# Order of the value products around the max pass, and one wider mask product, in a two-layer attention and MLP kernel

## What is computed

```python
# layer 1: 16 heads of 32 dimensions, causal, LoRA on q, k, v and o, rotary q and k
scores = where(causal, einsum('bhqd,bhkd->bhqk', Q, K) / sqrt(32), -inf)
x = layernorm(x + multilora(softmax(scores) @ V, Wo))
# layer 2: a second causal attention whose output only steers a small modulation of the gate
mod  = 0.1 * tanh(attention(rmsnorm(x, ln1_w)) @ A)
h    = rmsnorm(x, ln2_w)
gate = silu(h @ W_in.T + mod * (h @ A) @ B)
x    = layernorm(x + x + gate * (h @ W_up.T) @ W_down.T)
```

## Time and profile before

| | |
|---|---|
| median of 3 runs | 2931.94 us (2924.23 to 2940.3) |
| the profiled execution | 2926.47 us, its span 2924.6 us |
| mean granted TensorE clock | 0.965 |
| PE | 2691.6 us busy (92% of the span), 13840 matmuls |
| PEld | 2060.2 us (70%), 13840 loads |
| DVE / ACT / POOL | 1585.8 / 1337.3 / 647.0 us |
| first attention, first batch's first slot to last batch's last | about 72 to 834 us |
| second attention, likewise | about 932 to 1769 us |
| MLP | from about 1800 us on |

### The profile page before, as it was taken

How to read it: one execution, slowest core, us unless ns; L and a number is a source line. 1 busy time by engine, 2 the same in 40 slices (tenths; PEclk the granted TensorE clock), 3 DMA queues, 4 the chain that set the end, 5 groups by cost and what they waited for, 6 DMA issues and landing times. The chain is left out here.

```text
span 2924.6 us, 41449 instructions
## 1 busy us (share of the span) xinstructions
PE 2691.6 (92%) x13840; PEld 2060.2 (70%) x13840; DVE 1585.8 (54%) x4309; ACT 1337.3 (46%) x2755; POOL 647.0 (22%) x528
## 2 busy tenths in 40 slices
PE   5999999999758999999999984999999999999998
PEld 4777777777536667666666653888888888888886
DVE  4777777777635777777776773322222333333333
ACT  2677776767633666666666663211111231111111
POOL 5455555555321122222222111000000000000000
PEclk8999999999867999999999997999999999999999
DMA  5456555555625545555455444211111221111100
GB/s 141 94 132 140 134 127 133 134 131 120 151 85 124 120 97 133 115 104 138 105 111 129 99 76 136 96 45 45 44 44 44 77 84 53 45 46 44 44 29 29
DMA packets 173900, 276.47 MB, mean 95 GB/s; under 512 B 29204, under 2 KB 53524, under 8 KB 173076
## 3 DMA queue, kind: packets, MB, share of 16 engines
q1 hardware_dynamic: 170772, 260.58, 36.9%
q0 software_dynamic: 2304, 12.58, 1.2%
q10 hardware_dynamic: 640, 1.05, 0.1%
HBM read 97.04 MB, written 42.99 MB: 48 GB/s over the span
## 5 line engine op out<-in xcount | busy, mean ns | idle before, releaser
L2222 DVE TENSOR_TENSOR c_product<-c_up_ps,c_gate 128x512 f32<-128x512 f32 x128 | 88.5, 692 | 653.2 <-PE c_up_ps L2288 653.2
L2276 PE MATMUL c_gate_ps<-c_h_split,c_w_split 128*128 128x512 f32 x1536 | 380.3, 396 | 22.6 <-DVE c_w_split L2174 22.6
L2260 PE MATMUL c_down_ps<-c_w_split,c_product_split 128*128 128x512 f32 x1536 | 379.3, 396 | 0.0
L2288 PE MATMUL c_up_ps<-c_h_split,c_w_split 128*128 128x512 f32 x1536 | 378.1, 394 | 0.0
L2276 PEld LDWEIGHTS c_gate_ps<-c_h_split,c_w_split 128*128 128x128 f32 x1536 | 289.0, 188 | 94.8 <-issue 24.4
L2288 PEld LDWEIGHTS c_up_ps<-c_h_split,c_w_split 128*128 128x128 f32 x1536 | 287.9, 187 | 70.5
L2260 PEld LDWEIGHTS c_down_ps<-c_w_split,c_product_split 128*128 128x128 f32 x1536 | 288.5, 188 | 69.0
L278 ACT ACTIVATE b_prob_hi<-b_scores_t_ps 128x384 fp32r<-128x384 f32 (+1 forms) x384 | 200.3, 522 | 235.8 <-PE b_scores_t_ps L268 212.4
L286 DVE TENSOR_TENSOR a_prob_lo<-a_scores_t_ps,a_prob_hi 128x384 fp32r<-128x384 f32 (+1 forms) x384 | 226.5, 593 | 144.0 <-ACT a_scores_t_ps L279 141.3
L2146 ACT ACTIVATE c_gate<-c_gate_ps 128x512 f32<-128x512 f32 x128 | 76.7, 599 | 492.6 <-PE c_gate_ps L2283 492.6
L286 DVE TENSOR_TENSOR b_prob_lo<-b_scores_t_ps,b_prob_hi 128x384 fp32r<-128x384 f32 (+1 forms) x384 | 225.9, 593 | 136.9 <-ACT b_scores_t_ps L279 135.5
(11 more groups left out here) (206 smaller groups left out, 4789.2 us busy)
## 6 DMA issues: line engine op xcount, KB each, us to landing
a_q_stack<-a_q_split SPq DMA_DIRECT2D x192, 128.0 KB, 3.7
a_k_stack<-a_k_split SPq DMA_DIRECT2D x192, 128.0 KB, 3.8
b_q_stack<-b_q_split SPq DMA_DIRECT2D x192, 128.0 KB, 3.3
b_k_stack<-b_k_split SPq DMA_DIRECT2D x192, 128.0 KB, 3.6
c_h_stage<-h_t SPq DMA_DIRECT2D x16, 1024.0 KB, 6.1
c_res<-x SPq DMA_DIRECT2D x16, 1024.0 KB, 5.5
c_w_stage<-in_mlp_w POOLq DMA_DIRECT2D x16, 768.0 KB, 4.5
stage<-in_x_t SPq DMA_DIRECT2D x8, 1024.0 KB, 6.4
```

The costliest lines, as they stand in the source:

```text
L2222: dve.tensor_tensor(product[:, bank, :], up_ps[:, bank, :], gate[:, bank, :], ALU.mult).then_inc(product_done, 1)
L2260: mm = pe.matmul(down_ps[:, t, :], product_split[:, kt % 2, a, t * P:t * P + P], w_split[:, w, kt, 2 * KC * P:], start=(kt == 0 and i == 0 ...
L2276: pe.matmul(gate_ps[:, bank, :], w_split[:, w, ft, c * 2 * P:c * 2 * P + P], h_split[run.pair][:, a, c, :], start=(c == 0 and w == 0 and a ...
L2288: mm = pe.matmul(up_ps[:, bank, :], w_split[:, w, ft, c * 2 * P + P:(c + 1) * 2 * P], h_split[run.pair][:, a, c, :], start=(c == 0 and w = ...
```

## The change

It does two things in the first two stages.

1. `pv_unit` gets a range of passes. All matmuls of a value product but the last are issued directly behind the mask, the last behind the max-pass scores of that slot and ahead of the fill. The order of a unit's key tiles is turned round (`PV_PASSES`): for unit 2 first the two 128-wide matmuls, then the two 256-wide ones.
2. In unit 2 the two key tiles change places in the buffer, so that their diagonal blocks are neighbours; one mask matmul with 256 columns takes the place of two with 128. `colmask` is held twice side by side, at the price of one more DVE copy at the start.

```diff
-KEY_MAJOR = (((0, 0, 512),), ((1, 0, 384),), ((2, 0, 256), (3, 256, 128)))
+KEY_MAJOR = (((0, 0, 512),), ((1, 0, 384),), ((2, 128, 256), (3, 0, 128)))
+DIAGONAL = (P, P, 2 * P)
+PV_PASSES = tuple(tuple((kt, col, width, part) for kt, col, width in unit[::-1] for part in range(2))
+                  for unit in KEY_MAJOR)
...
-    for kt, col, width in KEY_MAJOR[j]:
-        mm = pe.matmul(at.scores_t_ps[:, k % 2, col:col + P], eye_bf[:, :], colmask[:, :],
-                       start=False, stop=True, skip_group_check=True)
-    mm.then_inc(at.score_t_ready, 1)
+    pe.matmul(at.scores_t_ps[:, k % 2, 0:DIAGONAL[j]], eye_bf[:, :], colmask[:, 0:DIAGONAL[j]],
+              start=False, stop=True, skip_group_check=True).then_inc(at.score_t_ready, 1)
...
                     score_t_unit(pe, at, eye_bf, colmask, b, g, slot)
+                    if slot >= 2:
+                        value_needed(b, g, slot - 2)
+                        pv_unit(pe, at, b, g, slot - 2, slice(0, -1))
+                    elif not first:
+                        pv_unit(pe, at, *group(b, g, -1), UNITS - 2 + slot, slice(0, -1))
                     if not (last and g == GROUPS - 1):
                         for k in score_share(slot):
                             score_unit(pe, at, *group(b, g, 1), k)
-                    if slot < 2 and not first:
-                        pv_unit(pe, at, *group(b, g, -1), UNITS - 2 + slot)
+                    if slot >= 2:
+                        pv_unit(pe, at, b, g, slot - 2, slice(-1, None))
+                    elif not first:
+                        pv_unit(pe, at, *group(b, g, -1), UNITS - 2 + slot, slice(-1, None))
...
-                    if slot >= 2:
-                        value_needed(b, g, slot - 2)
-                        pv_unit(pe, at, b, g, slot - 2)
```

More of the change, by code:

```diff
@@ L96, in __init__ @@
         self.eye_bf = sb("eye_bf", [P, P], BF16)
-        self.colmask = sb("colmask", [P, P], BF16)
+        self.colmask = sb("colmask", [P, 2 * P], BF16)
         self.lnw = sb("lnw", [P, 2, KC])
@@ L287, in lo_unit, with pv_unit @@
                       ALU.subtract).then_inc(at.lo_done, 1)
-def pv_unit(pe, at, b, g, k):
+def pv_unit(pe, at, b, g, k, passes=slice(None)):
     h, j = divmod(k, 3)
     n = number(b, g)
-    pe.wait_ge(at.lo_done, n * UNITS + k + 1)
-    if j == 0:
-        at_least(pe, at.pv_copied, n * GH + h - 1)
-    if g == 0 and h == 0 and at.value_steps:
-        pe.wait_ge(at.value_ready, b * at.value_steps[3] + at.value_steps[j])
-    for kt, col, width in KEY_MAJOR[j]:
-        for part, prob in enumerate((at.prob_hi, at.prob_lo)):
-            mm = pe.matmul(at.pv_ps[0:at.vcols, h % 2, kt * P:SEQ], at.value[:, kt, g * GH + h, :],
-                           prob[:, k % at.ring, col:col + width], start=(kt == 0 and part == 0),
-                           stop=(kt == TT - 1 and part == 1), skip_group_check=True)
-    mm.then_inc(at.pv_done, 1)
+    pv = PV_PASSES[j]
+    for kt, col, width, part in pv[passes]:
+        if (kt, col, width, part) == pv[0]:
+            pe.wait_ge(at.lo_done, n * UNITS + k + 1)
+            if j == 0:
+                at_least(pe, at.pv_copied, n * GH + h - 1)
+            if g == 0 and h == 0 and at.value_steps:
+                pe.wait_ge(at.value_ready, b * at.value_steps[3] + at.value_steps[j])
+        prob = (at.prob_hi, at.prob_lo)[part]
+        mm = pe.matmul(at.pv_ps[0:at.vcols, h % 2, kt * P:SEQ], at.value[:, kt, g * GH + h, :],
+                       prob[:, k % at.ring, col:col + width], start=(kt == 0 and part == 0),
+                       stop=(j == 2 and (kt, col, width, part) == pv[-1]), skip_group_check=True)
+        if (kt, col, width, part) == pv[-1]:
+            mm.then_inc(at.pv_done, 1)
 def pv_copy(act, at, b, g, h):
@@ L823, in _ @@
             dve.tensor_copy(eye_bf[:, :], square[:, 0, :]).then_inc(const_ready, 1)
-            dve.tensor_copy(colmask[:, :], square[:, 1, :]).then_inc(const_ready, 1)
+            for i in range(2):
+                dve.tensor_copy(colmask[:, i * P:(i + 1) * P], square[:, 1, :]).then_inc(const_ready, 1)
             def weights(n):
@@ L943, in _ @@
         def _(pe):
-            pe.wait_ge(const_ready, 3)
+            pe.wait_ge(const_ready, 4)
             pe.wait_ge(rows_zeroed, 4)
```

## The result

| | before | after |
|---|---|---|
| median | 2931.62 us of 6 runs (2924.23 to 2940.3) | 2909.63 us of 6 runs (2903.5 to 2917.16) |
| ratio after/before | | 0.9931, interval 0.9914 to 0.9949 |
| profiled execution (span) | 2926.47 us (2924.6) | 2913.56 us (2911.7) |

The change makes the kernel 22 us faster, 0.7%. The forecast was 31 us; 22 lie inside the range. The ratios in this document are those on record and not quotients of the medians (0.9925 here); the two differ by up to 0.001, 3 us.

What follows compares the result with a forecast made beforehand. PE was taken to set the pace. Of 47 us of PE work saved 30 arrive, less 5 for the later max pass, plus 4 and 2 for less waiting: 2931.9 - 31 = 2901 us, range 2883 to 2924 (8 in 10).

Steps and rivals of the forecast that it cites:

- Sign and mechanism: Both attentions: faster, chance 0.78, because a short matmul on PE hides only a narrow weight load.
- Rival 1: Masks on PE: the 0.12 us is the mask's own wherever it stands; 12 us gained, 2920; chance 0.1.
- rival 4: Weight loads on PE: every load is hidden, only the merged mask counts, 1 to 4 us, 2929; chance 0.03.
- Work taken from PE, 47 us: Both attentions: 3.65 us a batch less PE work in the first, 2.66 in the second; 25.6 and 21.3 us.
- The merged mask: Unit 2, both attentions: one 256-wide mask for two saves 0.015 us each, 0.24 us a batch.
- The later max pass, -5 us: Both attentions: max-pass scores come later, delaying DVE's maxima and low part; PE waits at about two places a batch.
- Rival 3: Slots 1 to 7: the later max pass becomes the bound, 76 us lost against at most 47 gained, 2961; chance 0.06.
- What of it arrives, 30 of 47 us: Saved PE work partly becomes waits: a third off the first attention (to 17), four tenths off the second (to 13).
- Rival 2: Both attentions: score buffers and DVE take the saved time back as low-part waits; 9 us gained, 2923; chance 0.1.
- Less waiting, +4 and +2 us: PE's max-pass scores wait less for DVE's buffer (second attention, 4); ACT less for finished heads (first, 2).
- the turning that was forecast: Unit 2's value product turned round and divided: 0.88 us a batch of PE work saved in either attention.

Runs made afterwards that it cites:

- Experiment 5: Changed kernel, but value products of three of four heads in the first attention load 128 columns of weights instead of 65: 2911.01 us, 0.9936 against before.
- repeat: The changed kernel unaltered, run and profiled again later, the same run as experiment 12: 2901.69 us, ratio 0.9923 against before.
- experiment 1: Kernel before with only the merged 256-column mask in unit 2, order of PE as before: 2920.2 us against 2926.04, ratio 0.9975.
- experiment 2: Changed kernel with two 128-wide masks in unit 2 instead of the merged one: 2903.11 us, 0.9924 against before.
- experiment 12: The changed kernel unaltered, measured again beside later runs on the same chip, called the repeat: 2901.69 us, ratio 0.9923 against before.
- experiment 3: Changed kernel with the whole value product ahead of the max pass in both attentions: 2907.55 us, 0.9933 against before.
- experiment 8: Changed kernel, but in slots with a max pass the whole value product stands behind the max-pass scores: 2916.65 us, 0.9943 against before.
- experiment 11: Changed kernel with only the gather of finished heads issued ahead of the next batch's load in the first attention: 2897.5 us, 0.9905 against before.
- Experiment 4: Changed kernel with the key tiles of a value product in their old order: 2912.53 us, 0.9953 against before.
- Experiment 9: Changed kernel, first attention: gather ahead of next batch's load, inverse sums written ahead of the low-rank rows and read back behind them: 2886.45 us, 0.9863 against before.

## Why the prediction was right, and where it wasn't

**Sign and mechanism: right.** The value products behind the mask take the 0.12 us of a mask to 0.07 or 0.08, "0.07 to 0.08 in all slots"; scores of 256 and 128 take 0.18 behind a 256-wide matmul; 13584 matmuls; the MLP alike. Experiment 5 shows the load to be the cause, with the mask unchanged ahead of it. Rival 1 falls, and rival 4 with it. That rule of the Trainium skill (TensorE: Matmul & The Clock Gate, Step-by-step: what each phase is for), that the next weights load while a matmul runs, holds here as far as the running matmul reaches: a 128-column load is hidden behind 256 columns, but 0.05 us of it stick out behind 128.

**Work taken from PE, 47 us: about right, a little high.** The busy time of PE fell by 35.8 us (after) and 41.5 us (repeat). Time gained and waits grown give about the same: in the first attention 9.5 + 7.1 + 3.6 = 20 of the 25.6 us forecast (19 in the repeat), in the second 11.8 + 7.4 = 19 of 21.3. In the two batches it fell by 2.1 and 1.7 us, at or just under the lower end of "2 to 3.5".

**The merged mask: without effect here.** It was counted at 0.24 us a batch, some 4 us in all, with the whole 0.06 a mask as its other bound. Alone it brought 6 to 7 us (experiment 1), on top of the order nothing that can be told (experiments 2 and 12): the 0.015 us saved a mask are 0.01 with the value's narrow load behind and 0.05 to 0.06 with a wide one, and the new order leaves only the first kind.

**The later max pass, -5 us: not settled.** Experiments 3 and 8 move it both ways, and both come out within 0.0012 of their expectations, which hold a price of this size; but so would a price of nothing. Rival 3, a loss of some 76 us, falls.

**What of it arrives, 30 of 47 us: the term that failed, and in the first attention.** The forecast took off what lies in slots around waits already seen, a third and four tenths. But slots that were just in time began to wait: PE's waits for low parts rose from 68 to 87 places in the second attention, and by 14.5 us in both. That is 0.9 us a batch, not "a few tenths", though under the 2 us at which the prediction would have been wrong. The keys' wait, named as a thing that could be late next, did become later, at the same place of the same batch from 0.95 to 2.13 us. Before, then after:

```profile
410.17 0.50 PE L182 MATMUL a_scores_ps<-a_k_stack,a_q_stack 112*128 112x512 f32 x1 [0.95 <-DMA a_k_stack<-a_k_split]
```

```profile
406.18 0.50 PE L185 MATMUL a_scores_ps<-a_k_stack,a_q_stack 112*128 112x512 f32 x1 [2.13 <-DMA a_k_stack<-a_k_split]
```

So 22 of 47 arrived, a little under half (with the terms for the later max pass and for less waiting, which no run separates, left at nothing): in the first attention 10 of 25.6 us where 17 were forecast (its batch was to take 93.2 us and took 95.0), in the second 12 of 21.3 where 13 were (105.5 forecast, 105.4 measured). Rival 2 was right in kind (the buffers take it back), not in size.

**Less waiting, +4 and +2 us: half right.** ACT's wait for heads fell by 22.7 us instead of vanishing, and 7.7 of it came back as the wait for the gather. In the second attention too the wait for heads turned into one for the gather. What either brought in time wasn't separated; experiment 11, which takes that gather wait away, gained 4 us on the repeat, within the intervals.

**Open.** The gain is 9 us smaller than forecast, inside the range. That the first attention lets only 0.4 of the saved work through is measured, but how its loss divides among low parts, keys and head copies is read from waits, not from a run that removes one of them on its own. Experiment 4 undid more than the turning that was forecast: it puts a 128-wide matmul ahead of wide weights twice a unit, 26 us of work, and 5 to 9 us came back. In the second attention the grown waits weren't divided between the two score buffers and DVE's order of work: no kernel with a third buffer was tried.

## What to carry to other kernels

Read PE's timeline from start to start, and put narrow weights behind short matmuls, wide weights behind long ones: here an order that adds and removes no work brought 0.7%. When PE is 93 to 95% busy, still expect only about half of what PE saves to arrive, since the other chains are just in time; after such a change look for the waits that grew, above all at DMA issues, where one move of a few lines brought another 15 us. Before moving an issue ahead in a queue, follow who waits for what it passes: the same keys sent ahead of a round trip cost 11 us, the round trip hidden under other issues gained. And look at the granted clock behind the waits that grew: part of those 11 us was PE at half clock.

## What the runs showed that I had not expected

A us taken from PE and a us taken from a DMA chain are worth different amounts in the same stage. Experiment 5 put 13.6 to 16.1 us of work back on PE in the first attention, and the stage grew by 2.5 to 5.0. Experiment 9 against 11 took 11.0 us from PE's wait for the keys (20.0 to 9.0), and the stage shrank by 12.4 (736.5 to 724.1), the median by 11.05 (2897.5 to 2886.45). PE is 93 to 95% busy there and still partly fills time that the chain from heads over sums and POOL to keys sets. Each stage is read from one profile, and two profiles of one program differ by 2.5 us, so the sizes are rough; the contrast is larger than that.

A round trip of a small array through HBM makes the issuing queue wait between its two issues: 1.9 us in the place shown (395.56 to 397.43), 38.9 us in 31 places over the first attention of after, 1.3 in the mean. The Trainium skill (DMA: Bandwidth & Descriptors, Anatomy of one DMA — SWDGE (gpsimd) path) puts a fixed cost of about 2.0 us on a DMA, for another way of issuing it; here the write of 8 KB takes 1.4 us from issue to landing (median of 31). What was new to me is that the queue's other issues can fill it.
